# Folding N through five PSUM banks instead of four in a fused attention and feed-forward kernel

## The reference, cut to what matters

```python
# x (16, 1024, 512); ctx (16, 64, 512); fs (16, 16); 16 heads of 64
ln = layernorm(layernorm(x), ln2_w, ln2_b)
q  = (ln @ Wq) per head * (1 + fs) + fs
k, v = split(layernorm(ctx, ln1_w, ln1_b) @ Wkv)
attn = softmax(q @ k.T / 8)                    # per head, over 64 context rows
x  = x + concat(attn @ v) @ Wout
x  = x + tanh(layernorm(x) @ weight @ aux1 @ aux2 + bias)
```

## Time and profile before

| what | value |
|---|---|
| runs | 2040.29, 2042.72, 2043.25 us (median 2042.72) |
| the profiled execution's own time | 2043.87 us |
| its span, first to last instruction | 2042.1 us |
| PE busy | 2027.2 us, 99% of the span |
| DVE, ACT, POOL busy | 75%, 65%, 66% of the span |
| mean granted TensorE clock | 0.999 |

### The profile page before, as it was taken

One profiled execution on the slowest core, in us unless ns is written; L12 is line 12 of the kernel. 1 busy time (PEld: TensorE's weight loads), 2 busy tenths in 40 slices (PEclk: granted clock), 3 DMA queues, 4 the chain that ended last, 5 costly groups with the idle time before them and its releaser, 6 DMA issues.

```text
span 2042.1 us, 31382 instructions
## 1 busy us (share of the span) xinstructions
PE 2027.2 (99%) x9180; PEld 1683.0 (82%) x9180; DVE 1525.3 (75%) x2414; ACT 1318.1 (65%) x3004; POOL 1350.0 (66%) x1467
## 2 busy tenths in 40 slices
PE   9999999999999999999999999999999999999998
PEld 7887878888888888888888888888888888888887
DVE  7677876776777777777777777777777778777776
ACT  5465766666766666666666666666666666666654
POOL 3146757677676767667676777767677676767564
PEclk9999999999999999999999999999999999999999
DMA  7758978888887887878688787878767676766653
GB/s 250 229 178 237 274 212 238 243 232 241 232 231 195 225 231 202 229 201 234 190 223 221 214 232 203 231 192 221 211 192 205 178 201 183 201 182 192 178 168 119
DMA packets 502491, 431.54 MB, mean 211 GB/s; under 512 B 54833, under 2 KB 408241, under 8 KB 502321
## 3 DMA queue, kind: packets, MB, share of 16 engines
q1 hardware_dynamic: 502320, 429.54, 75.4%
HBM read 251.33 MB, written 178.06 MB: 210 GB/s over the span
## 4 chain that ended last, share of the span: by engine, by line
PE 82%; DVE 3%; ACT 3%; SPq 2%; issue 2%; DMA 2%; POOL 2%; DVEq 0%; ACTq 0%; POOLq 0%
PE bank L161 33%; PE bank L1192 20%; PE bank L166 16%; PE bank L1195 10%; DMA m_scratch<-evac 1%; PE bank L895 1%; PE bank L894 1%; POOL area L1474 1%; POOL area L1481 1%; DVE turned L1357 1%; DVE area L1335 1%; DVE row_max L1340 0%; ACT bank L1008 0%; ACT pT_hi L1243 0%; SPq L835 0%
## 5 line engine op out<-in xcount | busy, mean ns | idle before, releaser
L1474 POOL TENSOR_TENSOR area<-area,row_max 128x256 f32<-128x256 f32 x512 | 353.9, 712 | 153.6 <-DVE row_max L1340 153.6
L1192 PE MATMUL bank<-N_hi,pT_hi 128*128 128x512 f32 x1024 | 398.7, 389 | 1.2 <-DVE N_lo L1003 0.8
L161 PE MATMUL bank<-M_hi,xT_hi 128*128 128x512 f32 x1024 | 398.7, 389 | 0.0
L161 PE MATMUL bank<-M_lo,xT_hi 128*128 128x512 f32 x1024 | 398.7, 389 | 0.0
L1192 PE MATMUL bank<-N_lo,pT_hi 128*128 128x512 f32 x1024 | 398.6, 389 | 0.0
L1243 ACT CAST pT_hi<-turned 128x512 fp32r<-128x512 f32 x256 | 159.1, 621 | 336.6 <-DVE turned L1357 336.6
L1498 POOL TENSOR_TENSOR area<-area 128x512 f32<-128x512 f32 x127 | 166.4, 1310 | 286.7 <-ACT area L1282 286.5
L1481 POOL TENSOR_TENSOR area<-area,row_inv 128x512 f32<-128x512 f32 x256 | 269.2, 1052 | 106.5 <-DVE row_inv L1349 106.5
L1346 DVE TENSOR_REDUCE row_sum<-area 128x8 f32<-128x512 f32 x256 | 174.4, 681 | 166.2 <-ACT area L1238 165.3
L1366 DVE TENSOR_TENSOR pT_lo<-turned,pT_hi 128x512 fp32r<-128x512 f32 x256 | 199.8, 780 | 120.3 <-ACT pT_hi L1243 120.3
L166 PE MATMUL bank<-M_hi,xT_lo 128*128 128x512 f32 x1024 | 273.7, 389 | 0.0
(11 more groups left out here) (184 smaller groups left out, 3926.5 us busy)
## 6 DMA issues: line engine op xcount, KB each, us to landing
p_scratch<-area SPq DMA_DIRECT2D x256, 256.0 KB, 2.6
p_moved<-p_scratch SPq DMA_DIRECT2D x512, 128.0 KB, 4.3
area<-x_dram SPq DMA_DIRECT2D x128, 256.0 KB, 4.7
area<-x_turned_dram SPq DMA_DIRECT2D x128, 256.0 KB, 4.0
x_scratch<-area SPq DMA_DIRECT2D x127, 256.0 KB, 3.0
x_moved<-x_scratch SPq DMA_DIRECT2D x508, 64.0 KB, 3.5
y_dram<-area SPq DMA_DIRECT2D x127, 256.0 KB, 3.7
land<-m_scratch SPq DMA_DIRECT2D x120, 256.0 KB, 2.8
```

Of the source, the lines that this page charges most:

```text
L161: mm = eng.matmul(ps, sh, mv, start=(n == 0), stop=False)
L1192: pe.matmul(O_ps[:], st(pT_hi, k), n_cols(mv, k), start=(k == 0 and mv is N_hi), stop=False)
L1474: last = pool.tensor_tensor(s, s, row.to_broadcast([P, 2, 4, J2]), ALU.subtract)
```

## The change

The rotation of the fold in slots 9, 17, ..., 121 gets a fifth bank, `O_ps` (bank 6), so the banks of products 0 to 7 are 0, 1, 2, 3, 6, 0, 1, 2 where they were 0, 1, 2, 3, 0, 1, 2, 3. Product 4 no longer waits for the `N_lo` of product 0 but for `s_x2`, VectorE's reading of `O_ps` in the same slot. Products 5, 6, 7 wait for the `N_lo` of products 0, 1, 2 instead of 1, 2, 3 (through `len(use)` in `fold_n_pe`). The waits behind the fold move with the last user of each bank: the scores of slot t+1 wait for the `N_lo` of products 5 and 6 (halves q = 0 and 1) instead of 4 and 5; the first half of p @ N for that of product 4 instead of 3, since product 4 now lies in the bank that p @ N overwrites; tile 28 for that of product 7 instead of 6. No instruction that computes is added or removed.

```diff
-        first_fold_ps, fold_ps = [banks[i] for i in (2, 3, 7)], banks[0:4]
+        first_fold_ps, fold_ps = [banks[i] for i in (2, 3, 7)], banks[0:4] + [O_ps]
...
             if n == 28:
-                pe.wait_ge(s_nl, 8 + 7)
+                pe.wait_ge(s_nl, 8 + 8)
...
                     elif m == 2 and t > 2:
-                        pe.wait_ge(s_nl, t + 3 + q)
+                        pe.wait_ge(s_nl, t + 4 + q)
                     scores_pe(pe, t, q)
...
                     if m == 2:
-                        pe.wait_ge(s_nl, u + 4 + 4 * q)
+                        pe.wait_ge(s_nl, u + 5 + 3 * q)
...
                     if t == TPB + 1 and p == 2:
                         pe.wait_ge(s_tsum, 27)
+                    if p == 4:
+                        pe.wait_ge(s_x2, t - 1)
                 fold_n_pe(pe, t - 1, range(8), free)
```

## The result

The changed kernel took 2047.3 us (median of 9 runs, 2045.07 to 2049.28) where the kernel before took 2042.72; ratio 1.0023, 95% interval 1.0014 to 1.0031. (One of the nine runs of the kernel before beside it took 2327.59 us and does not count in the ratio.) Measured again later it was 1.0018 (1.0010 to 1.0027). Both intervals exclude no change. The two ratios are +4.7 and +3.7 us; the forecast was +2.3 (2045.0), with a range of 2042.2 to 2047.6. The profiled execution took 2047.78 us, its span is 2046.0.

A forecast was written before the change was run, and what follows sets the result against it. PE, busy 99% of the span, was taken to bound the kernel. Gains of 0.95, 0.23 and 0.27 us in slots 9, 17 and 25 against 3.7 lost in twelve later folds gave +2.3, 2045.0 us; range 2042.2 to 2047.6.

The forecast's parts named there:

- Where the time goes: Folds of slots 33 to 121: no wait inside to remove, so waits added at the scores decide.
- Size of this term: Scores behind the twelve folds of slots 33 to 121: second matmul 0.31 us later each, 3.7 us lost in all.
- The price: Scores after a short wait: second matmul starts 0.34 us after release, so 0.31 us lost; bounds 0.20 and 0.42.
- Slot 9: Product 4 runs early, product 5 waits for product 0's N_lo, three products remain after it; gain 0.95 us.
- a fall of the clock: Slot 9 after PE's wait: a stretch mixing 2.4 and 1.2 GHz, costing 1.6 us; taken as recurring after the change.
- Slots 17 and 25: Wait inside the fold goes, scores wait for product 5's N_lo instead; gains 0.23 and 0.27 us, together 0.5.
- the D piece: Piece of M's folding between fold and scores in slots 17 and 25, 0.48 us, hiding part of the scores' wait.
- the 1.45 us of forecast gains: Gains of 0.95 us in slot 9, 0.23 in slot 17 and 0.27 in slot 25.
- the rival in which the fall of the clock is missing in the timed runs before: Slot 9: timed runs before lack the fall, so slot 9 loses 0.3; net +3.5 us, 2046.2; chance 0.17.
- The rival of a clock that falls after short waits: Twelve later slots: each new wait brings a 1.2 GHz stretch costing 1.6 us; +19, about 2064; chance 0.03.
- a slack of 0.26 us to a lack of 0.42: Slot 33 scores, weight load due 647.03: N_lo released at 646.77 with four banks, 647.45 with five, 0.42 us late.

The follow-up runs named there:

- The wait alone: Kernel before, four banks kept, only the wait of the scores behind the fold raised by one product (N_lo of products 5 and 6); ratio 1.0023.
- five banks from slot 33 on: Changed kernel, but slots 9, 17 and 25 keep four banks and their old waits; five banks only from slot 33 on; ratio 1.0023.
- slot 9 only: Changed kernel, but five banks (0, 1, 2, 3, 6) only in the fold of slot 9, four in all others; ratio 1.0003.
- the order 2, 3, 6, 0, 1: Changed kernel with its five banks reordered so banks 0 and 1 serve only products 3 and 4, after mending a slot 2 wait; ratio 0.9988, 2040.67 us.
- the changed kernel once more: Repeat of the changed kernel, no edit, timed beside the kernel before; ratio 1.0018.

## Why the prediction was right, and which terms were off

- **Where the time goes: right.** The twelve folds of slots 33 to 121 had nothing to give and lose at the scores behind them. The first matmul moved by 0.20 and the second by 0.31, as worked out. "The wait alone" and "five banks from slot 33 on" each give the loss by themselves.
- **Size of this term: 3.7 forecast, 4.3 in the trace.** 0.36 us a fold, not 0.31. The missing 0.05 stands behind the second matmul: there the profile after has starts 0.23, 0.24, 0.23 us apart (647.37, 647.60, 647.84, 648.07 in the timeline), several of them 0.236 instead of 0.227. The price was read up to the second matmul only. The trace before had the rest at one of its waits: in slot 25 the last matmul of the fold starts 2.66 us after the released one (525.12 to 527.78), in slot 17 2.61 (401.89 to 404.50), which is 0.34 + 10 x 0.227.
- **Slot 9: mechanism right, value not.** The `N_lo` of product 0 is released at a time of VectorE's own, product 4 is done ahead, three are left. From that release to the scores' second matmul the forecast was 281.86 - 277.95 = 3.91 us with a fall of the clock and 3.34 without; the profiles have 3.98 (slot 9 only, with a fall: 279.51 to 283.49) and 3.32 (changed kernel: 279.65 to 282.97). So both cases exist. What the forecast left out is that the release itself moves: it comes 6.09 and 6.29 us after the start of the fold in the two profiles before, 5.96 and 5.00 in the two after. Taken was a fall on both sides and a gain of 0.95. The profile pairs give 1.3 instead of it (4.66 against 3.32), but the timed runs of "slot 9 only" show +0.6 us, within -1.2 to +2.5.
- **Slots 17 and 25: right in kind.** The waits inside went, the scores' wait came, and the D piece covers a part. The forecast gain of 0.5 stands against 0.8 in the first pair of profiles (246.11 to 245.28) and against a loss of 1.0 in the second (245.62 to 246.58), which is the scatter of slot 25's lateness.
- **Sum.** The central value was low by half; the mechanism of the loss and the range held. In the traces the later folds lose 4.3 us; of the 1.45 us of forecast gains the timed runs show none. The measured +3.7 to +4.7 lies nearest to the rival in which the fall of the clock is missing in the timed runs before (+3.5); the two corrections, 0.6 for the later folds and up to 1.2 for slot 9, bring +2.3 to +4.1. But that rival does not hold as it was put. The fall stands in five of five profiles with four banks and without added matmuls in slot 9. Of 93 timed runs of the kernel before whose mean granted clock is listed, 20 list 0.998 (mean 2044.6 us) and 12 list 1.000 (mean 2040.9), the other 61 0.999, which leaves it open; so some have a fall and some have none. Of 20 of the changed kernel two list 1.000 and none 0.998. How the shares of the two kernels compare, and so what slot 9 is worth in timed runs, stays open: the tests of that part resolve no less than 1.7 us.
- **The rival of a clock that falls after short waits did not come.** Twelve waits of 0.20 us left the granted clock at 1.00. What the Trainium skill (TensorE: Matmul & The Clock Gate, "A second HAM failure mode: psum-queue depth-cycling") reports of another kernel, a clock that goes up and down with frequent idle moments between groups of matmuls, did not occur here, with one such wait in every eighth slot. What more frequent waits would do no run here shows.

## What to carry to other kernels

When a buffer is added to a ring, ask who comes next after the ring, not only who waits inside it: one more bank shifts which product is last in each bank, and here the next user's wait moved from a slack of 0.26 us to a lack of 0.42. Let the buffers that the next stage needs be those that the ring uses once: the order 2, 3, 6, 0, 1 turned the same fifth bank from +0.2% into -0.12%. Waits shorter than a printed matmul don't appear in a list of PE's waits; compare the starts of matmuls, or a long stretch of many periods between two profiles.

## What the runs showed of the hardware

- A short wait of PE costs more than its length: in the twelve later folds the first matmul is 0.20 us late, the second 0.31, and what follows 0.36 (4.3 us over twelve folds).
- After a standstill of about 2 us the clock may or may not fall. The same gap, 277.26 to 279.65 in the changed kernel and 277.12 to 279.51 with five banks in slot 9 only, was followed by 2.4 GHz in the one execution and by 1.2 GHz in the other. A gap of 275.21 - 272.92 = 2.29 us between starts was enough for a fall. With matmuls issued into the gap the clock stayed at 2.4 GHz in the profiles of both kernels that did so.
- The wait of PE inside the fold of slot 25, between 0 and 1.9 us, goes together with a DMA: in the profile of "slot 9 only", ScalarE stood still three times ahead of that fold until a store of a folded tile had left its buffer (timeline of ACT):

```profile
484.86 0.59 ACT L923 COPY evac<-bank 128x512 f32<-128x512 f32 x1 [2.52 <-DMA m_scratch<-evac]
...
499.65 0.59 ACT L923 COPY evac<-bank 128x512 f32<-128x512 f32 x1 [1.22 <-DMA m_scratch<-evac]
...
515.66 0.59 ACT L923 COPY evac<-bank 128x512 f32<-128x512 f32 x1 [1.36 <-DMA m_scratch<-evac]
```

The third of these stops stands in three of the twelve profiles: this one, the changed kernel once more (1.17 us) and "from slot 33 on" (1.19). They are the three with the longest waits of PE in that fold, 1.85, 0.97 and 1.65 us; in the nine others that wait is 0.72 or less. That it is the cause was read from the traces, not tested.
